# Moving one addition of a recurrent state from VectorE to GpSimd in the joint steps of two interleaved scans

## The reference

```python
def cell(h, x):                       # layer 1, state h of (8, 512)
    gi = x @ W_ih + b_ih
    gh = h @ W_hh + b_hh
    r = sigmoid(i_r + h_r); z = sigmoid(i_z + h_z)
    n = tanh(i_n + r * h_n)
    h_new = (1.0 - z) * n + z * h
...
def _derivative(q, p, drive, coupling, bias):   # layer 2, q and p of (8, 512)
    i_couple = tanh(q) @ coupling.T
    dq = q - q ** 3 / 3.0 - p + drive + i_couple + bias
    dp = EPSILON * (q + ALPHA - BETA * p)
# four evaluations of it in each step, each needing the one before
```

## Time and profile before

| what | value |
|---|---|
| median of 3 runs | 5117.64 us (5112.13 to 5129.14) |
| profiled execution | 5103.12 us |
| its span | 5101.5 us |
| GpSimd busy over the span | 298.2 us (6%), 867 instructions |
| VectorE busy over the span | 2819.2 us (55%), 16412 instructions |
| mean granted clock of TensorE | 0.78 |

### The profile page before, as it was taken

The page is one execution under the profiler, slowest core; times in us unless marked ns, Lnnn a source line. Parts: engine busy times, 40 slices in busy tenths (PEclk is TensorE's granted clock), DMA queues, the critical chain, the costliest instruction groups (busy, mean ns, idle before and its releaser), DMA issues. The chain is left out here.

```text
span 5101.5 us, 196672 instructions
## 1 busy us (share of the span) xinstructions
PE 4800.1 (94%) x83696; PEld 3821.7 (75%) x83696; DVE 2819.2 (55%) x16412; ACT 1521.0 (30%) x6006; POOL 298.2 (6%) x867
## 2 busy tenths in 40 slices
PE   8899989799999999999997599999989999999999
PEld 3335654599999999999996587889979999444434
DVE  4110011479999999999998735675553432344421
ACT  1100111234444444444443322233322222233330
POOL 1010010001111111111111100000000000000000
PEclk7899999655555555555555599999989999999999
DMA  2202430000000000000001000034320000100000
GB/s 83 102 35 80 169 125 17 15 4 5 5 5 5 5 5 5 5 5 5 5 5 53 3 20 1 2 86 99 93 85 3 3 3 3 45 9 8 8 8 33
DMA packets 52290, 159.57 MB, mean 31 GB/s; under 512 B 13873, under 2 KB 14001, under 8 KB 46272
## 3 DMA queue, kind: packets, MB, share of 16 engines
q1 hardware_dynamic: 45408, 130.70, 7.8%
q0 software_dynamic: 3712, 12.29, 0.7%
q10 hardware_dynamic: 2304, 4.20, 0.2%
HBM read 129.63 MB, written 17.17 MB: 29 GB/s over the span
## 5 line engine op out<-in xcount | busy, mean ns | idle before, releaser
L621 PE MATMUL k_ps<-k_hl,k_wlo 128*128 128x8 f16 x16384 | 607.2, 169 | 141.1 <-ACT k_hl L697 136.7
L621 PEld LDWEIGHTS k_ps<-k_hl,k_wlo 128*128 128x128 f16 x16384 | 533.6, 105 | 177.3 <-ACT k_hl L697 160.3
L625 PE MATMUL k_ps<-k_hl,k_whi 128*128 128x16 f16 x16384 | 588.7, 174 | 0.0
L625 PEld LDWEIGHTS k_ps<-k_hl,k_whi 128*128 128x128 f16 x16384 | 516.1, 104 | 0.5
L621 PE MATMUL g_ps<-g_hl,g_wlo 128*128 128x8 f16 x12288 | 436.8, 168 | 41.3 <-DVE g_hl L775 37.2
L625 PE MATMUL g_ps<-g_hl,g_whi 128*128 128x16 f16 x12288 | 441.5, 174 | 0.0
L621 PEld LDWEIGHTS g_ps<-g_hl,g_wlo 128*128 128x128 f16 x12288 | 387.1, 104 | 47.5 <-DVE g_hl L775 42.6
L697 ACT ACTIVATE k_hl<-k_q 128x32 f16<-128x32 f32 x768 | 175.9, 229 | 742.5 <-DVE k_q L732 742.5
L625 PEld LDWEIGHTS g_ps<-g_hl,g_whi 128*128 128x128 f16 x12288 | 387.1, 104 | 0.0
L1446 DVE TENSOR_REDUCE t_NM<-t_ps 128x1 f32<-128x512 f32 x256 | 165.0, 686 | 211.9 <-PE t_ps L1312 211.9
L1218 DVE TENSOR_TENSOR HQ<-p_ior,p_pm 128x2048 f32<-128x2048 f32 x64 | 146.3, 2290 | 223.9 <-PE p_sim L1042 223.9
(11 more groups left out here) (328 smaller groups left out, 8902.0 us busy)
## 6 DMA issues: line engine op xcount, KB each, us to landing
GRZ<-expert_places SPq DMA_DIRECT2D x64, 512.0 KB, 4.9
wm<-in_w_dram SPq DMA_DIRECT2D x4, 2816.0 KB, 10.4
GRZ<-in_w_dram SPq DMA_DIRECT2D x4, 2816.0 KB, 10.3
m_w<-in_w2a_dram SPq DMA_DIRECT2D x8, 1280.0 KB, 12.6
GRZ<-in_ue_dram SPq DMA_DIRECT2D x8, 1024.0 KB, 7.6
GRZ<-in_x_nat_dram SPq DMA_DIRECT2D x4, 1024.0 KB, 10.5
XT<-in_xT_dram SPq DMA_DIRECT2D x1, 4096.0 KB, 27.0
expert_rows<-wm SPq DMA_DIRECT2D x1, 4096.0 KB, 24.1
```

The source lines that it names most:

```text
L621: T.matmul(P[:,j,1,:],lo[:,kc,(m0+j)*128:(m0+j+1)*128],x[:,kc,0,:],start=(j==0 and kc==0),stop=False,skip_group_check=True)
L625: i=T.matmul(P[:,j,:,:],hi[:,kc,(m0+j)*128:(m0+j+1)*128],x[:,kc,:,:],start=False,stop=kc==KC-1,skip_group_check=True)
```

## The change

In the joint steps the full-precision state of GRU step `s-1` is no longer added by VectorE after `k_Q` but by GpSimd, between its `k_E` and its `drive`. `upd` now counts up a semaphore `g_m` of its own, on which GpSimd and VectorE's `state_half` wait; `diff` waits in addition for `g_h`, since the row it reads can come from GpSimd. In the 32 steps of the GRU alone VectorE keeps the addition.

```diff
-g_h=sem('g_h')
+g_h=sem('g_h'); g_m=sem('g_m')
...
@@ gpsimd
             for t in range(NT):
                 e.wait_ge(k_p,t+1); e.wait_ge(k_D,t+1)
                 G.tensor_tensor(E0[:],D[:],p[:],ALU.subtract).then_inc(k_u,1)
+                s=t+LEAD-1
+                if t>0 and s<NT:
+                    e.wait_ge(g_m,s+1); e.wait_ge(g_th,s+1)
+                    G.tensor_tensor(HS[:,(s//TL)%2,:,s%TL,:],m4(mm_[:]),m4(n[:]),ALU.add).then_inc(g_h,1)
                 if t+1<NT: drive(t+1)
@@ vector
             def diff(s):
                 if s>=NT: return
                 e.wait_ge(g_th,s+1)
+                if s>0: e.wait_ge(g_h,s)
...
             def upd(s):
                 if s>=NT: return
                 e.wait_ge(g_sz,s+1); ch.after(at['d'])
-                at['m']=ch.did(V.tensor_tensor(mm_[:],zg[:],dd[:],ALU.mult))
+                V.tensor_tensor(mm_[:],zg[:],dd[:],ALU.mult).then_inc(g_m,1)
             def state_half(s):
                 if s>=NT: return
-                ch.after(at['m'])
+                e.wait_ge(g_m,s+1)
...
             def state_full(s):
                 if s>=NT: return
-                ch.after(at['m'])
+                e.wait_ge(g_m,s+1)
...
                 n_Q=ch.did(stt(Q[:,0,:],E0[:],a,q[:,0,:]))
-                if t>0: state_full(s-1)
                 n_G=ch.did(stt(G0[:],p[:],-BETA,q[:,0,:]))
```

More of the change, by code:

```diff
@@ L591, in scan @@
         s_c=sem('in_cond'); s_lw=sem('in_lora'); s_i=sem('init')
-        g_hi=sem('g_hi'); g_lo=sem('g_lo'); g_mm=[sem(f'g_mm_{x}') for x in 'rzn']; g_ar=sem('g_ar'); g_az=sem('g_az'); g_sr=sem('g_sr'); g_sz=sem('g_sz'); g_w=sem('g_w'); g_th=sem('g_tanh'); g_hS=sem('g_hS'); g_h=sem('g_h')
+        g_hi=sem('g_hi'); g_lo=sem('g_lo'); g_mm=[sem(f'g_mm_{x}') for x in 'rzn']; g_ar=sem('g_ar'); g_az=sem('g_az'); g_sr=sem('g_sr'); g_sz=sem('g_sz'); g_w=sem('g_w'); g_th=sem('g_tanh'); g_hS=sem('g_hS'); g_h=sem('g_h'); g_m=sem('g_m')
         l_h=sem('l_h'); l_ht=sem('l_ht'); l_tr=sem('l_tr'); l_hm=sem('l_hm'); l_o=sem('l_o'); l_x=sem('l_x')
```

## The result

The changed kernel is slower: a median of 5151.00 us over 12 runs (5136.66 to 5161.61) against 5122.98 us for the kernel before over 12 runs in the same comparison (5105.44 to 5137.49). The ratio is 1.0058, 95% interval 1.0046 to 1.0070; the medians lie 28 us apart. The forecast was 5112.6 us in a range up to 5124. The profiled execution has a span of 5150.3 us.

The account below looks back on a forecast made before the run. The prediction took the oscillators' chain of evaluations to bound the kernel. It summed 56 x 0.09 = 5.0 us won and nothing for all other terms, giving 5117.6 - 5.0 = 5112.6 us, range 5095 to 5124.

Parts of the forecast that it names:

- What bounds the kernel: Joint steps: the chain of the oscillators' four evaluations sets the pace, 7.35 us a step; GRU work fills its gaps.
- TensorE's price: From the start of line 625's matmuls to `k_v`: 0.61 us when TensorE, not VectorE, is what releases `k_v`.
- the 56 steps: Joint steps without expert or router matmuls before stage 0: VectorE late there, 0.09 us each to win, 5.0 us in all.
- the 0.02 of stage 3: Stage 3: VectorE always a little late, `k_v` 0.63 us after line 625 where TensorE alone would give 0.61.
- The addition leaves VectorE: Stage 0: one VectorE slot of 0.10 us freed ahead of `k_v`; 5.0 us won, bounds 4.5 to 7.3, at most 22.4.
- The addition on GpSimd: Stage 0: takes 0.26 us, starts 0.25 behind `upd`, with 0.4 us of cover before `low` needs it.
- Contention: GpSimd working amid VectorE's order in stage 0: nothing put for it, as the trace showed the copy overlapping line 825 without effect.
- Cost nothing: GpSimd's queue: `drive` and the copy move later behind the new wait, but their readers come much later; no cost.
- sign of a lock: Profile after: a hole on VectorE between `upd` and `cubic` growing beyond today's would show the forecast wrong.
- the other 168: Joint steps with expert or router matmuls before stage 0: TensorE sets `k_v`, so the freed slot wins 0.
- the 0.02 of slack: Stage 0 after expert matmuls: VectorE is only 0.02 us ahead of being late itself.
- The rival of the lock: Stage 0: GpSimd's addition blocks line 825 for up to 0.26 us; 36 us slower, 5153 us; chance 0.05.

Follow-up runs that it names:

- the gaps: Kernel before, with the last `k_B` of stage 0 and `diff` moved between `k_v` and `k_q`: 5112.13 us, ratio 0.9983; second time 5115.15 us, 0.9990.
- the extra addition: Kernel before, plus one GpSimd addition of two constant 128x32 tiles per joint step, behind the copy, its result unused: 5132.45 us, ratio 1.0016.
- Drive late: Kernel before, VectorE keeping the state addition, but GpSimd's `drive` waits for the product of `upd`: 5148.08 us over 8 runs, ratio 1.0052.
- the long memset: Kernel before, plus one GpSimd memset of a 128x256 scratch tile per joint step, behind the copy: 5119.75 us, ratio 0.9994.

## Why the prediction was wrong

*What bounds the kernel*: right. `k_v` sets the pace, TensorE's price is 0.61 us, VectorE was late in the 56 steps, by 0.08: there `k_v` stood 0.69 behind line 625 in the median step, and the gaps brought it to 0.61. These steps became 0.07 and 0.06 us shorter in the mean in the two runs of the gaps, of the 0.08 and the 0.02 of stage 3; where the rest went stays open.

*The addition leaves VectorE*: right in kind. A slot is 0.10 us, and behind the holds `k_G` moved up by it. `k_S` moved up by 0.09 only: with the addition gone it stands 0.21 behind the `k_Q` that it waits for.

*The addition on GpSimd*: 0.253 us and 0.27 behind `upd`, as sized (0.26, 0.25), and `low` never waited for it.

*Contention: "So I put nothing for it."* This is the step that failed: the term is 0.25 us in each step, in three holds. The argument was that the copy runs across the start of line 825 in the earlier trace rows with no effect. It starts at 1513.20 and ends at 1513.44; `low_part` is issued at 1513.34 and lasts to 1513.53 anyway. A hold until 0.05 after GpSimd's end would be over at 1513.49 and could not show. In stage 3 (kernel before, just ahead of the earlier trace rows) `k_D` starts just after `diff`, and the instruction after that, `k_v`, has an input in PSUM:

```profile
1512.41 0.18 DVE L767 TENSOR_TENSOR g_d<-g_HS,g_n 128x32 f32<-128x32 f32 x1
1512.47 0.26 POOL L716 TENSOR_TENSOR k_D<-XT,k_bias 128x32 f32<-128x32 f32 x1
1512.51 0.18 DVE L732 SCALAR_TENSOR_TENSOR k_v<-k_ps,k_S 128x32 f32<-128x32 f32 x1
```

`k_E` (line 721) runs beside two instructions of gate z with an input in PSUM and is over 0.02 us before `diff` is issued. So in no joint step of the kernel before did a GpSimd instruction start ahead of a VectorE instruction with two SBUF inputs and outlast it; the rows could not speak against a hold. The even 252 ns of line 721 say nothing either, as the lengthening falls on VectorE. The line of the half-precision addition beside the extra addition (235 ns for 188) shows that a longer overlap would have been seen.

*"Cost nothing" for the moved `drive` and copy*: the second step that failed, by the same fault. Only their readers were asked for, not what they would run against. Drive late, alone, costs 23.3 us in the joint stretch; with the state addition moved and `drive` left where it was it is 6.3. The prediction's own sign of a lock, a hole between `upd` and `cubic` that grows, is there: from 0.51 us to 0.71 between their starts in the median step.

The sum that the runs give for the changed kernel, in stage 0: each hold is counted by how much later the next instruction starts, 0.09, 0.11 and 0.05 us. Less the slot of 0.10, and with the 0.01 of `k_S` and about as much at `low`, it is 0.16 to 0.17; measured 0.16 at `k_v` in the median of the 56 steps (1.42 to 1.58 behind the clip). In the other 168 the 0.02 of slack of the earlier trace rows is taken off, and in those where the expert matmuls end later still, more: in 14 of them line 625 starts 1.03 behind the clip, and `k_v` does not move. The mean over all steps is 0.134, and 224 x 0.134 = 30 us, for 30.8 measured.

The rival of the lock had 0.16 and 36 us, against 28 by the medians and 30.8 in the joint stretch, with a chance of 0.05, which was far too little. That its 5153 us stand so near to 5151 is luck in part: it started from a median of 5117.6, which came out at 5123.0 over 12 runs, and it counted one hold of 0.26 where there are three short ones, of which it named the second only in passing.

The durations of the joint steps give the hold a plain form. A VectorE instruction with two SBUF inputs that is issued while GpSimd's is under way ends at its own time or a little behind GpSimd's recorded end, whichever is later. Behind a GpSimd addition of two SBUF tensors it is 0.04 to 0.05 us, be the held instruction `low_part`, the half-precision addition, `cubic`, `k_G` or `diff`. Behind the copy, which has one input, it is 0.01 to 0.02 us.

The Trainium skill, in "SBUF — State Buffer", section "Who interferes with whom", has the rule: a VectorE instruction with two inputs in SBUF contends with a GpSimd instruction that reads SBUF, and the order of issue decides who blocks. All runs here agree on which pairs collide: reading and not writing (0.188 us beside the long memset, 0.235 beside an addition), two SBUF inputs and not one in PSUM (0.24 for `diff`, 0.18 for `k_v`), and the order of starting (0.28 for `low_part` when it came 0.02 second, 0.19 when 0.03 first). The same section has the second one blocked for the whole of the first, and this the runs do not show. A `low_part` that came 0.03 first would have cost GpSimd's addition 0.16 us up to its recorded end, and it cost 0.02; and `cubic`, issued in the last 0.03 us of an addition, was not held at all.

Not settled: why the end of a hold lies further behind an addition than behind a copy (two inputs against one would fit, but no run varied that alone), and whether VectorE instructions with one SBUF input and none in PSUM are held; no run tried these.

## What to carry to other kernels

Before an instruction is moved to GpSimd, look at which VectorE instructions with two SBUF inputs will be issued while it, and every instruction queued behind it on GpSimd, is under way; each of them was held here to its end or just behind it, where it would have ended sooner by itself. An overlap in the trace is evidence against such a hold only if GpSimd's instruction starts first and ends no sooner than VectorE's would have. Where an engine's slot ahead of a critical instruction is the cost, a gap that the engine spends waiting for its own result is the cheaper place for it.

## What the runs showed of the hardware

VectorE's 128x32 instructions start 0.10 us apart while each lasts 0.18, and an instruction that waits for the one before it starts 0.21 to 0.23 behind it; so one more fits in between for nothing, as `k_B` does in the gaps. GpSimd's start 0.21 us apart with durations of 0.25, and 0.25 to 0.27 behind the start of the VectorE instruction that releases them. When VectorE's `low_part` started first, GpSimd's addition was lengthened by only 0.02 us (0.277 against 0.253 us), far less than the 0.16 that `low_part` still ran by its record.
